# Two causal attentions: value copies moved in the queue, a new order within the turn, a copy moved to GpSimd, and two extra products in steps without a small task

## The reference

```python
att = jnp.einsum('bhqd,bhkd->bhqk', q, k) * scale
att = jnp.where(causal[None, None], att, -jnp.inf)
att = jax.nn.softmax(att, axis=-1)
out = jnp.einsum('bhqk,bhkd->bhqd', att, v)
out = out.transpose(0, 2, 1, 3).reshape(B, T, C)
return jnp.einsum('btc,dc->btd', out, Wo)
```

## Time and profile before

| | |
|---|---|
| median of 3 runs | 2356.11 us (2355.21 to 2358.67) |
| the profiled execution's own time | 2360.74 us |
| its span, first to last instruction | 2359.0 us |
| mean granted clock of PE | 0.879 of full |
| PE, DVE, ACT, POOL busy | 83%, 68%, 38%, 19% of the span |
| first attention, turns 0 to 7 | 85.6 to 412.5 us |
| second attention, turns 0 to 7 | 1739.7 to 2061.9 us |

### The profile page before, as it was taken

One profiled execution on the slowest core, in us unless ns is written; L12 is line 12 of the kernel. 1 busy time (PEld: TensorE's weight loads), 2 busy tenths in 40 slices (PEclk: granted clock), 3 DMA queues, 4 the chain that ended last, 5 costly groups with the idle time before them and its releaser, 6 DMA issues. The chain is left out here.

```text
span 2359.0 us, 28355 instructions
## 1 busy us (share of the span) xinstructions
PE 1966.9 (83%) x9864; PEld 1246.2 (53%) x9864; DVE 1593.2 (68%) x3414; ACT 904.7 (38%) x1689; POOL 455.7 (19%) x320
## 2 busy tenths in 40 slices
PE   7999999699999988856766386546899999999997
PEld 4543443488888856433433243323354444369997
DVE  4676773544445344779999999997368786356775
ACT  2365665222222222431112111101437665546765
POOL 1011111623133030001001100110001111115765
PEclk9788888899999999878887698777879996889999
DMA  6032321311110010200000000000203232128885
GB/s 178 13 65 46 77 48 33 125 36 54 36 53 18 0 54 9 79 1 10 10 1 8 18 9 9 0 0 4 60 15 66 54 77 42 33 87 247 233 222 119
DMA packets 60158, 132.73 MB, mean 56 GB/s; under 512 B 18952, under 2 KB 29960, under 8 KB 57216
## 3 DMA queue, kind: packets, MB, share of 16 engines
q1 hardware_dynamic: 50688, 118.17, 18.5%
q0 software_dynamic: 8832, 12.16, 3.0%
q10 hardware_dynamic: 512, 0.79, 0.2%
HBM read 91.27 MB, written 10.98 MB: 43 GB/s over the span
## 5 line engine op out<-in xcount | busy, mean ns | idle before, releaser
L779 DVE CUSTOM_DVE_ANT_0 pair<-pair,a_mask 128x512 f32<-128x512 f32 (+3 forms) x768 | 408.4, 587 | 174.9 <-PE pair L596 172.4
L751 ACT ACTIVATE a_prob<-pair 128x512 f32<-128x512 f32 (+3 forms) x768 | 329.3, 490 | 208.1 <-PE pair L622 203.7
L622 PE MATMUL pair<-a_qx,a_kx 50*128 50x512 f32 (+3 forms) x768 | 273.8, 457 | 8.6 <-ACT a_prob L751 7.5
L596 PE MATMUL pair<-a_kx,a_qx 48*128 48x512 f32 (+3 forms) x768 | 268.5, 437 | 14.6 <-DVE a_mx_raw L779 8.5
L622 PEld LDWEIGHTS pair<-a_qx,a_kx 50*128 50x128 f32 x768 | 131.6, 210 | 220.4 <-ACT a_prob L751 125.1
L636 PE MATMUL pair<-a_prob,a_v 128*17 128x512 f32 (+3 forms) x1536 | 189.7, 569 | 34.0 <-ACT a_o_all L756 28.6
L544 POOL TENSOR_SCALAR_AFFINE_SELECT a_prob<-a_prob 128x512 f32<-128x512 f32 x128 | 89.4, 699 | 649.1 <-ACT a_prob L751 648.8
L1016 DVE TENSOR_TENSOR m_h<-pair,m_g 128x512 f32<-128x512 f32 x96 | 66.4, 691 | 210.7 <-PE pair L839 209.5
L1398 PE MATMUL pair<-h_stream,r_w_kz 128*128 128x512 f32 x192 | 103.9, 695 | 118.7 <-DVE r_region L1804 113.4
L837 PE MATMUL pair<-m_x_hi,m_w_lo 128*128 128x512 f32 x448 | 178.4, 398 | 26.3 <-POOL m_w_lo L901 24.1
L838 PE MATMUL pair<-m_x_hi,m_w_hi 128*128 128x512 f32 x448 | 177.2, 395 | 0.0
(11 more groups left out here) (314 smaller groups left out, 4110.2 us busy)
## 6 DMA issues: line engine op xcount, KB each, us to landing
mx_raw<-in_L_ffn_experts SPq DMA_DIRECT2D x69, 512.0 KB, 4.7
m_raw<-in_L_cond_experts SPq DMA_DIRECT2D x18, 1024.0 KB, 4.9
a_qx<-a_comp SPq DMA_DIRECT2D x104, 96.0 KB, 2.8
a_kx<-a_comp SPq DMA_DIRECT2D x48, 192.0 KB, 4.4
a_factor<-a_inverses SPq DMA_DIRECT2D x56, 128.0 KB, 2.7
r_w_ring<-in_r_q_w SPq DMA_DIRECT2D x8, 512.0 KB, 3.9
m_raw<-in_L_cond_experts SPq DMA_DIRECT2D x6, 512.0 KB, 3.6
token_rows<-mx_h_rows SPq DMA_DIRECT2D x2, 1040.0 KB, 7.7
```

Source lines behind the costliest of these rows:

```text
L596: nc.tensor.matmul(first_bank[t % FR][:, 0:c1 - c0], qx[r, m % 2, a // 2, i * P:(i + 1) * P], kx[r, m % 3, a // 2, c0:c1], start=True, sto ...
L622: nc.tensor.matmul(score_bank[t % SR][:, q0:TT], kx[r, n % 3, a // 2, j * P:(j + 1) * P], qx[r, n % 2, a // 2, h * TT + q0:(h + 1) * TT], ...
L751: nc.scalar.activation(prob[:, i % RING, a, q0:TT], score_bank[t % SR][:, q0:TT], ACT.Exp, scale=SCALE).then_inc(s["b_exp"], 1)
L779: nc.vector.tensor_tensor_reduce(out=first_bank[t % FR][:, 0:cols], in0=first_bank[t % FR][:, 0:cols], in1=mask[:, m0:m0 + cols], scale=1. ...
```

## The change

Four things are edited, all in the two calls of `attention`.

1. **Copies.** ("copy", n, 0) and ("copy", n-1, 1) are no longer put where they were, but right after the next "scores" entry that follows their `values`. `VALUES_AFTER` changes in steps 0 (0 to 1) and 4 (2 to 1): copy (n, 0) is now queued after the scores of (4, 2), where it was after (5, 0); copy (n-1, 1) after the scores of (0, 2), where it was after (0, 0).
2. **Order.** `FIRSTS_AFTER` is another table with the same 48 firsts (by step 5, 4, 3, 3, 4, 6, 5, 5, 4, 3, 4, 2, where they were 4, 5, 3, 3, 4, 6, 5, 5, 4, 3, 5, 1), and `NORM` puts the norm steps at 2, 5, 8, 10, 11 in place of 3, 5, 8, 9, 10.
3. **Twin.** The 512-wide copy within SBUF leaves ACT's queue and goes to POOL, which now walks through `ORDER` as well; two of the three `memset`s of `kx` are issued after the second and third twin. The `memset` of `v_sb` has a semaphore of its own.
4. **Extra products.** In each step that has no small task (steps 1, 2, 3 and 7 to 11) of the turns 0 to 6, PE computes WARM = 2 products of 48 rows by 512 columns from `kx` into the shared bank; nobody reads them. They are queued last in the step and wait until the shared bank's last reader is done.

```diff
@@ -228,14 +228,15 @@
+WARM = 2
-FIRSTS_AFTER = ((2, 0, 1, 1), (2, 2, 0, 1), (1, 0, 2, 0), (0, 3, 0, 0),
-                (1, 0, 2, 1), (2, 2, 1, 1), (2, 0, 3, 0), (1, 2, 0, 2),
-                (2, 0, 1, 1), (0, 3, 0, 0), (1, 2, 0, 2), (0, 0, 1, 0))
-VALUES_AFTER = (0, 3, 3, 3, 2, 0, 1, 2, 3, 3, 2, 3)
+FIRSTS_AFTER = ((0, 2, 0, 3), (1, 3, 0, 0), (1, 2, 0, 0), (0, 0, 3, 0),
+                (2, 1, 1, 0), (3, 1, 2, 0), (2, 0, 2, 1), (2, 0, 1, 2),
+                (2, 0, 1, 1), (1, 0, 2, 0), (1, 1, 1, 1), (2, 0, 0, 0))
+VALUES_AFTER = (1, 3, 3, 3, 1, 0, 1, 2, 3, 3, 2, 3)
...
-NORM = {3: 0, 5: 1, 8: 2, 9: 3, 10: 4}
+NORM = {2: 0, 5: 1, 8: 2, 10: 3, 11: 4}
...
+    copies = []
     for i in range(NS):
         for a in range(GH):
             order.append(("scores", n, i, a))
+            order += copies
+            copies = []
...
             if a == VALUES_AFTER[i] and i:
                 order.append(("values", n, i - 1))
+                copies = [("copy", n, 0)] if i == 4 else []
             elif a == VALUES_AFTER[i] and n:
-                order += [("values", n - 1, NS - 1), ("copy", n - 1, 1)]
-            if (i, a) == (5, 0):
-                order.append(("copy", n, 0))
+                order.append(("values", n - 1, NS - 1))
+                copies = [("copy", n - 1, 1)]
...
+        if not closing and not small:
+            order.append(("warm", n, i))
...
+WARM_AFTER = {e: sum(x[0] in SHARED for x in ORDER[:n]) for n, e in enumerate(ORDER) if e[0] == "warm"}
...
-                for x in range(3):
+                def ones(x):
                     nc.gpsimd.memset(kx[:, x, :, :].bitcast(F32), 1.0).then_inc(s["ones"], 1)
+                def twin(m, h):
+                    pool.wait_ge(s["hi"], m * HALF + h + 1)
+                    to = parts(m)[:, :, half(h)].bitcast(F32)
+                    nc.gpsimd.tensor_copy(to[:, 0, :], to[:, 2, :]).then_inc(s["twin"], 1)
+                    if m * HALF + h in (1, 2):
+                        ones(m * HALF + h)
...
+                ones(0)
...
+                does = {"qk": twin, "scores": select}
+                for what, *which in ORDER:
+                    if what in does:
+                        does[what](*which)
...
+                def warm(n, i):
+                    pe.wait_ge(s["used"], WARM_AFTER["warm", n, i])
+                    for x in range(WARM):
+                        nc.tensor.matmul(shared_bank[0], kx[0:PRODUCT, n % 3, 0, 0:P], kx[0:PRODUCT, n % 3, 1, 0:TT],
+                                         start=True, stop=True)
...
-                    act.wait_ge(s["hi"], m * HALF + h + 1)
-                    nc.scalar.activation(to[:, 0, :], to[:, 2, :].bitcast(F32), ACT.Copy).then_inc(s["twin"], 1)
```

More of the change, by code:

```diff
@@ L331, in turn @@
                 uses = [] if what == "begin" else finished(*entry)
-    order += uses
+    order += uses + copies
     assert closing or found == NF
@@ L372, in attention @@
         "mask", "proj", "hi", "twin", "k_first0", "k_first1", "q_first0", "q_first1", "k_in", "q_in0", "q_in1", "m_in0", "m_in1", "used", "vp", "v_used", "a_mm",
-        "a_max", "m_hi", "m_lo", "t_mm", "b_mm", "b_exp", "b_cut", "pv", "o_sum", "o_cp", "o_spread", "n_out", "n_in", "n_rcp", "n_back", "n_wide", "n_done", "packed", "ones", "ow", "om")}
+        "a_max", "m_hi", "m_lo", "t_mm", "b_mm", "b_exp", "b_cut", "pv", "o_sum", "o_cp", "o_spread", "n_out", "n_in", "n_rcp", "n_back", "n_wide", "n_done", "packed", "ones", "v_ones", "ow", "om")}
     banks = [*c.quad, *[bank[:, :] for bank in c.bank]]
@@ L531, in _, with select @@
             def _(pool):
-                for x in range(3):
+                def ones(x):
                     nc.gpsimd.memset(kx[:, x, :, :].bitcast(F32), 1.0).then_inc(s["ones"], 1)
-                nc.gpsimd.memset(v_sb[:, :, :, :].rearrange("p x t (a s) -> p (x t a) s", s=VW)[:, :, HD:VW], 1.0)\
[L535 to L546, removed]
+                def twin(m, h):
[4 more added lines that the diff above has]
+                        ones(m * HALF + h)
+                def select(n, i, a):
+                    h, j = STEPS[i]
+                    if a < GH - 1 or j < 4 * h:
+                        return
+                    pool.wait_ge(s["b_exp"], (n * NS + i + 1) * GH)
+                    q0 = cut(h, j)
+                    block_ = prob[:, i % RING, :, q0:q0 + P]
+                    nc.gpsimd.affine_select(out=block_, in_=block_, compare_op=ALU.is_ge, fill=0.0, base=0,
+                                            pattern=[[0, GH], [1, P]], channel_multiplier=-1)\
+                        .then_inc(s["b_cut"], 1)
+                ones(0)
+                nc.gpsimd.memset(v_sb[:, :, :, :].rearrange("p x t (a s) -> p (x t a) s", s=VW)[:, :, HD:VW], 1.0)\
+                    .then_inc(s["v_ones"], 1)
+                does = {"qk": twin, "scores": select}
+                for what, *which in ORDER:
+                    if what in does:
+                        does[what](*which)
             @block.tensor
@@ L614, in scores @@
                     if n == 0 and i == 0 and a == 0:
-                        pe.wait_ge(s["ones"], 3 + 1)
+                        pe.wait_ge(s["ones"], 3)
+                        pe.wait_ge(s["v_ones"], 1)
                         pe.wait_ge(s["v_used"], NG)
@@ L693, in _ @@
                 does = {"qk": qk_projection, "v": v_projection, "first": first, "max": maxima, "scores": scores,
-                        "values": values, "sums": sums, "spread": spread, "out": out_projection, "begin": begin_out}
+                        "values": values, "sums": sums, "spread": spread, "out": out_projection, "begin": begin_out, "warm": warm}
                 for what, *which in ORDER:
```

## The result

The changed kernel takes 2334.15 us (median of 20 runs, 2321.41 to 2355.64) against 2355.66 us for the kernel before (20 runs, 2336.75 to 2405.91): ratio 0.9921, 95% interval 0.9895 to 0.9947. It is faster by 0.8%. The prediction said 2291, 2.8% faster, with a range up to 2340.

The account below looks back on a forecast made before the run. PE was taken to bound attention where its clock is half, DVE close behind at full clock. From 2360.7 us, -25.9 (gap) - 60 (clock) + 20.6 (products) = -65 gave 2295, as a median 2291; range over all cases 2260 to 2340.

Parts of the forecast that it names:

- The clock term: Attention turns: with the gap gone, 142 of 170 winnable us at half clock are won, 60 us; bounds 0 and 82.
- The rate: Attention turns: 0.42 us lost for each us PE is at half clock, from turns of 40.9 and 35.1 us.
- one sixth: Share of the 170 us at half clock left unwon, for falls with no such gap in front of them.
- The products' term: 224 extra products on PE: cost 20.6 us, six per turn at 0.215 us, ten in steps 7 to 11 free; bounds 0, 96.
- The gap: PE's idle wait before step 4's values products, until ACT's copy: moving the copies gains 25.9 us in turns 0 to 6.
- The order: New order of firsts and norm DMAs: cost 0, bounds 1 us a turn either way, 14 each.
- The twin: 512-wide copy moved from ACT to POOL, priced 0.5 us there: cost 0, bounds -1 and +4.
- B: Rival: half of the 170 us stays at half clock, falls in steps 0 to 3 or 8 to 11; 2328, chance 0.20.
- A: Rival: products are ballast; removing the gap alone holds the clock, every product costs full price; 2307, chance 0.15.
- C: Rival: products load a PE that stays at half clock, costing 65 us against 25.9 of gaps; 2395, chance 0.09.
- The forecast's own range: 2262 to 2315: low end all 170 us won at 0.48 with 12 us products' cost (-96), high end products at 48.
- the range over all cases: 2260 to 2340 for the whole kernel: takes in the forecast and two rivals, leaves out the two slower ones.

Follow-up runs that it names:

- e8: Changed kernel with four extra products per step in place of two (448 in all); 2459.28 us, ratio 1.0434.
- e7: Kernel before with the copies moved, plus the new table of firsts and norm places (twin on ACT, no products); 2326.69 us, ratio 0.9928.
- e5: Kernel before with the copies moved, plus two extra products in step 11 and two in step 0 of turns 0 to 6; 2323.79 us, ratio 0.9898.
- e3: Kernel before with the extra products alone, copies not moved; 2392.64 us, ratio 1.0110.
- e9: Changed kernel with its extra products in steps 1, 2 and 3 alone (six per turn); 2370.03 us, ratio 1.0076.
- e13: Changed kernel with extra products in steps 1 to 3 alone, but in turn 0 also in steps 7 to 11; 2292.26 us, ratio 0.9783.
- e14: Changed kernel with extra products in steps 7 to 11 alone, but in turn 0 in steps 1 to 3 instead; 2300.9 us, ratio 0.9819.
- e1: Changed kernel without its 224 extra products; copies, order and twin as changed; 2323.1 us, ratio 0.9824.
- e2: Kernel before with the two copies moved, nothing else (twin on ACT, no products); 2302.92 us, ratio 0.9760.
- e12: Kernel before with copies moved and twin on POOL, plus 17 single 128-row products per attention before and early in turn 0; 2348.15 us, ratio 1.0018.

## Why the prediction was wrong

- **The clock term failed.** "I take five sixths as won, 142 x 0.42 = 60 us" was 72 x 0.42 = 30 us. The rate held: turn 3 of the changed kernel lost 7.0 us to 17.1 us at half clock, 0.41. The step under it, that the falls stand behind the gap and go with it, was right for those falls (none of the changed kernel's turns falls behind a wait for the copy). What it missed is that full clock is not the state that remains: the clock also falls about 3 us after a turn's start, where there is no gap, in some turns and not in others of the same work. The prediction had seen such a fall, which it puts at the end of the second attention's turn 5 (at 1977.9 in rows 4, 0.7 us into turn 6), and sized it with one sixth. And the number of falls does not follow from the work added: 62 to 349 us in kernels with 0 to 32 products a turn, 294 and 62 with the same turns 1 to 6.
- **The products' term was too small where I costed nothing.** "Ten of a turn's 16 products are there and I cost them at nothing" was 1.04 us a turn. In steps 1 to 3 the 1.29 us were 1.01. Together 2.03 a turn, 28 us over 14 turns against 20.6, and more where the clock is at half. The full-clock turn is 35.07, not 34.3. Doubling the products (e8) cost 3.5 us a turn more, so the second sixteen were dearer than the first. Two of them in a row on PE (L665), with a first (L616) beside:

```profile
142.10 0.49 PE L665 MATMUL pair<-a_kx 48*128 48x512 f32 x1
142.11 0.50 PE L616 MATMUL pair<-a_kx,a_qx 48*128 48x512 f32 x1
...
142.21 0.19 PEld L665 LDWEIGHTS pair<-a_kx 48*128 48x128 f32 x1
...
142.44 0.39 PE L665 MATMUL pair<-a_kx 48*128 48x512 f32 x1
```

  They start 0.34 us apart, not 0.215, but the first of a pair can run beside a first of another head. Of the 112 pairs in this profile 80 start 0.34 us apart at full clock, the 14 of step 7 start 0.23 apart, and the 18 at half clock 0.59. The prediction halved 0.43 from rows 8; the pair before it in the same rows starts 0.60 us earlier (196.44 to 197.04). The rule of the Trainium skill that the prediction used (TensorE: Matmul & The Clock Gate, Part 3, What overlaps and what doesn't) is stated there of weight loads: one overlaps with matmuls in flight only when its row group differs. For the products these rows agree with the prediction's reading: the pair does not run side by side, and the neighbour on the other rows starts 0.01 us after it. For the loads they don't agree: the second L665's load is recorded 0.11 us after the first product's start, on the same rows.
- **The gap was right**: 25.9 us said; turn 1 of the second attention, at full clock, is 1.94 us shorter with the copies alone, and there were 14 gaps.
- **The order was costed at nothing**, 1 us either way: 0.75 us a turn won at full clock, inside the bounds, and with the twin on ACT more than lost in falls (e7). **The twin** at nothing: right, 0.61 us on POOL.
- **By turns**: 1 to 5 won 28.9 us (394.1 to 365.2), turns 0 5.3, the closing ones 1.3, and turns 6 lost 6.1: they were at half clock for much of their length before (51 us together) and still are (55), and pay for the products there. That is 29.4.
- **Rivals.** B, "the clock falls elsewhere", at 2328 and 0.20, is what happened, nearly to the place ("steps 0 to 3"). Its reason, narrow products in these steps, is not shown: with products added around the turn's start (e5) the falls came at 8.3 us instead. A's core, that the products do not pay, is shown as well: without them the kernel is 11 us faster (0.9824 against 0.9921; intervals 0.9771 to 0.9878 and 0.9895 to 0.9947). A was wrong that the clock then holds. C is refuted for the changed kernel, and its price of 65 us was 35.4 in e3, where the time at half clock did stay; that the clock gets worse with more products happened with four a step (e8).
- **The range.** The forecast's own range does not come out of its sums: -96 gives 2260, not 2262, and the products at 48 us give 2318, not 2315. The measured time lies outside it either way, and inside the range over all cases.

What stays open: what in the stretch before a fall decides. Busy time doesn't, and the products' number doesn't. That something ahead of a turn does is shown by e9 and e13 alone, one pair. That it is the moment at which the turn starts is the likely reading, and e14 came out against a simple form of it. The products do hold some clock in the changed kernel: its median granted clock is 0.889 in 20 runs against 0.874 in e1's six, which over the whole program is 521 against 585 us at half clock. At 0.42 the 64 us are worth 27 us, an estimate, about what the products cost at full clock (28); at half clock they cost more, and the medians say 11 us lost in all.

The best versions are e2 (only the copies) and e13. I would keep e2: 2302.92 us, 2.4% under the kernel before, with nothing in it that computes for no use. e13's 2292.26 hangs on what turn 0 does, and any edit ahead of the turns may shift it in the same way.

## What to carry to other kernels

Find the one wait in front of a clock fall, and move what it waits for in its own queue before adding anything: here that alone gave 2.4%, and with all other parts of the change 0.8% were left. The products gave some back, the order too where it was tried alone, and of the twin nothing was resolved. Where a loop's turns repeat with the same length, the clock can fall in each or in none, by what went before the first one; so compare versions by the full-clock length of a turn and by the mean granted clock of several runs, and don't credit a clock effect from one profile. Price filler work on a pipelined engine by the distance of two starts next to the very neighbours it will have.

## What the runs showed of the hardware that was not expected

- PE was shown busy 47.66 of 47.80 us at half clock (e12). The page of the Trainium skill on the clock gate (TensorE: Matmul & The Clock Gate, Part 1, The HAM clock gate) has activity release the throttle; these rows show no release by busy time.
- 48-row and 128-row products in turn start 0.72 us apart at half clock (e12), pairs of 48-row ones 0.59 (the changed kernel). The Trainium skill (TensorEngine Tiling (Array Packing), Key Properties) says that changing the tiling mode drains the engine; no run here measures a drain. The weight load of 0.29 us that the profile records with each of e12's products, and the 0.43 us of rows 8, already add up to 0.72.
- Twenty unused products more made the program 78 us faster (e9 to e13), and the clock fell in twelve of the twelve turns 1 to 6 (e9) or in one (e13), with the same work in them.
